# Both third-layer sums of a group added on VectorE, in place of a copy on ScalarE and an addition on GpSimd

## What is computed

```python
x = x + _L0_conv_ref(_ln_c(x), ...)          # sign convolution, batch norm, clip to -1..1
t = _to_tokens(x)                            # one token of 64 channels per point
t = t + _L0_ffn_ref(_ln_t(t), ...)
# inside the second:
w = jax.nn.softmax(feat @ Wr + br, axis=-1)  # feat: mean over the batch
h = relu(_bn(einsum('bfd,edh->bfeh', x, W1) + b1, ...))
h = relu(_bn(einsum('bfeh,ehk->bfek', h, W2) + b2, ...))
y = einsum('bfeh,ehd->bfed', h, Wo) + bo
return einsum('bfed,fe->bfd', y, w)
```

## Time and profile before

| | |
|---|---|
| median of three runs | 1410.8 us |
| the profiled execution | 1413.79 us, span 1411.7 us from the first to the last instruction |
| mean granted TensorE clock | 0.979 of full speed |
| instructions | 36466 |
| DMA | 107.41 MB, mean 76 GB/s |

### The profile page before, as it was taken

The page is one execution under the profiler, slowest core; times in us unless marked ns, Lnnn a source line. Parts: engine busy times, 40 slices in busy tenths (PEclk is TensorE's granted clock), DMA queues, the critical chain, the costliest instruction groups (busy, mean ns, idle before and its releaser), DMA issues.

```text
span 1411.7 us, 36466 instructions
## 1 busy us (share of the span) xinstructions
PE 1326.0 (94%) x14782; PEld 678.3 (48%) x14782; DVE 888.2 (63%) x1592; ACT 868.5 (62%) x1151; POOL 551.2 (39%) x474
## 2 busy tenths in 40 slices
PE   5798946999999999999999999999999999999998
PEld 3675732554444455445444444544454444444443
DVE  3343452666666767666666676667766677766655
ACT  4566654666666666666666666666666666666643
POOL 6104003444434444434444443444443444443441
PEclk9999966999999999999999999999999999999999
DMA  9977512233332323332233333233333232333121
GB/s 200 183 174 163 105 21 53 60 67 74 73 80 48 67 61 74 74 80 52 62 73 67 74 73 61 61 66 67 74 74 74 53 65 62 74 73 77 25 53 28
DMA packets 251026, 107.41 MB, mean 76 GB/s; under 512 B 238865, under 2 KB 239089, under 8 KB 250865
## 3 DMA queue, kind: packets, MB, share of 16 engines
q1 hardware_dynamic: 249600, 103.49, 34.9%
q0 software_dynamic: 1264, 1.61, 0.6%
HBM read 78.97 MB, written 26.09 MB: 74 GB/s over the span
## 4 chain that ended last, share of the span: by engine, by line
PE 92%; issue 3%; DMA 2%; DVE 1%; SPq 1%; ACT 1%; POOL 0%; POOLq 0%; DVEq 0%; ACTq 0%
PE ps L567 25%; PE ps L583 25%; PE ps L545 25%; PE ps L513 7%; PE ps L601 3%; PE ps L498 3%; PE ps L609 2%; PE ps L634 2%; DMA xa<-in_x 2%; PE ps L621 1%; PE ps L628 0%; SPq L266 0%; DMA spread<-rs_rows 0%; DVE bn L872 0%; ACT xc L753 0%
## 5 line engine op out<-in xcount | busy, mean ns | idle before, releaser
L908 DVE SCALAR_TENSOR_TENSOR v<-ps,negb,wb 128x448 f32<-128x448 f32 x896 | 571.0, 678 | 307.4 <-PE ps L567 306.2
L738 ACT ACTIVATE h<-ps,bias 128x896 f32<-128x896 f32 x448 | 451.5, 1008 | 332.1 <-PE ps L545 332.1
L545 PE MATMUL ps<-xc,w 64*64 64x448 f32 x3584 | 468.7, 542 | 15.2 <-POOL xc L422 11.3
L567 PE MATMUL ps<-h,w 64*64 64x448 f32 x3584 | 465.8, 541 | 5.6 <-issue 3.2
L583 PE MATMUL ps<-v,wo 64*64 64x448 f32 x3584 | 466.3, 539 | 3.7 <-issue 2.9
L583 PEld LDWEIGHTS ps<-v,wo 64*64 64x64 f32 x3584 | 179.1, 133 | 179.9 <-issue 160.6
L545 PEld LDWEIGHTS ps<-xc,w 64*64 64x64 f32 x3584 | 165.2, 132 | 189.6 <-issue 182.7
L567 PEld LDWEIGHTS ps<-h,w 64*64 64x64 f32 x3584 | 174.6, 133 | 161.9 <-issue 141.5
L452 POOL TENSOR_TENSOR o<-o,upper 128x448 f32<-128x448 f32 x112 | 127.3, 1137 | 299.8 <-DVE o L918 299.8
L444 POOL TENSOR_TENSOR o<-xin,gconst 128x448 f32<-128x448 f32 x112 | 130.6, 1186 | 235.9 <-ACT gconst L781 143.0
L422 POOL TENSOR_TENSOR xc<-xc,spread 128x896 f32<-128x896 f32 x56 | 123.5, 2221 | 209.9 <-DMA spread<-rs_rows 209.7
(11 more groups left out here) (143 smaller groups left out, 676.6 us busy)
## 6 DMA issues: line engine op xcount, KB each, us to landing
xa<-in_x SPq DMA_DIRECT2D x64, 392.0 KB, 7.4
xin<-in_x SPq DMA_DIRECT2D x112, 224.0 KB, 4.1
spread<-rs_rows SPq DMA_DIRECT2D x112, 224.0 KB, 4.1
out<-o SPq DMA_DIRECT2D x224, 112.0 KB, 2.5
rs_rows<-rs SPq DMA_DIRECT2D x112, 3.5 KB
rows<-in_L_ffn_g POOLq DMA_DIRECT2D x2, 256.0 KB, 12.9
rows<-in_L_ffn_v POOLq DMA_DIRECT2D x2, 256.0 KB, 14.8
cwt<-in_L_conv_weight SPq DMA_DIRECT2D x2, 144.0 KB, 2.7
```

What stands on the lines that cost most here:

```text
L545: last = mm(ps[64 * two:64 * two + 64, L1_BANKS + ab, 0:NG], w1[half, P * q + C * two:P * q + C * two + C], xc[half, s, g // 2, ab ^ (g % ...
L567: last = mm(ps[64 * i:64 * i + 64, L2_BANKS[ab] + low, 0:NG], w2[rows_, Q + QUADS * i, :], h[rows_, u % 2, i, ab, :], start=True, stop=True)
L738: A(h[:, u % 2, i], ps[:, L1_BANKS:L1_BANKS + 2, 0:NG], ACT.Relu, bias=bias[:, 0, q:q + 1]).then_inc(h_done[i], 1)
L908: last = V.scalar_tensor_tensor(out=v[:, u % 2, ab, d, :].rearrange("p (b w) -> p b w", w=W), in0=ps[:, L2_BANKS[ab] + d, 0:NG].rearrange( ...
```

## The change

VectorE now makes both additions of a group, one behind the other, the second behind a semaphore of its own (`lower_in`), since it reads what the first wrote. The ScalarE copy, the tile `upper`, the GpSimd addition and the semaphores `upper_done` and `sum_done` are gone. `out_done` counts the second addition, and TensorE and SyncE wait for it alone. GpSimd keeps `add_const`, `norm` and `feature`.

```diff
@@ store (SyncE)
-                    sp.wait_ge(sum_done, G * k + g + 1)
+                    sp.wait_ge(out_done, G * k + g + 2)
@@ GpSimd
-                def add_upper(k, g):
-
-                    pool.wait_ge(upper_done, G * k + g + 2)
-                    pool.wait_ge(out_done, G * k + g + 2)
-                    og = o[:, BG * g:BG * g + BG, :].rearrange("p b w -> p (b w)")
-                    nc.gpsimd.tensor_tensor(og, og, upper[:], ALU.add).then_inc(sum_done, 1)
-
                 def chunk(k, s, first, left):
-                    for g in range(G - 1):
+                    for g in range(G):
                         add_const(k, s, g)
-                    if not first:
-                        add_upper(k - 1, G - 1)
-                    add_const(k, s, G - 1)
-                    add_upper(k, 0)
                     if left:
                         for p in range(STEPS):
                             norm(k + 1, 1 - s, p)
                         feature(k + 1, 1 - s)
-                    add_upper(k, 1)
-                    add_upper(k, 2)
-                    if not left:
-                        add_upper(k, G - 1)
@@ layer3 (TensorE)
                         if Q == 0:
                             pe.wait_ge(out_done, G * k + g + 1)
-                            pe.wait_ge(upper_done, G * k + g + 1)
@@ ScalarE
-                def take_upper(k, g):
-                    act.wait_ge(l3_done, UNITS * k + QUADS * g + QUADS + RING2)
-                    if not (isinstance(k, int) and k == 0 and g == 0):
-                        act.wait_ge(sum_done, G * k + g)
-                    A(upper[:], ps[:, ACC_BANKS + 1, 0:NG], ACT.Copy).then_inc(upper_done, 1)
@@ add_out (VectorE)
-                    V.tensor_tensor(og, ps[:, ACC_BANKS, 0:NG], og, ALU.add).then_inc(out_done, 1)
+                    V.tensor_tensor(og, ps[:, ACC_BANKS, 0:NG], og, ALU.add).then_inc(lower_in, 1)
+                    dve.wait_ge(lower_in, G * k + g + 1)
+                    V.tensor_tensor(og, ps[:, ACC_BANKS + 1, 0:NG], og, ALU.add).then_inc(out_done, 1)
```

More of the change, by code:

```diff
@@ L113, in metaformer_kernel @@
         vareps = sb("vareps", [P, NG], F32)
-        upper = sb("upper", [P, NG], F32)
         placed = sb("placed", [C, PAIRS * 2, W], F32)
@@ L196, in metaformer_kernel @@
         l3_done = sem("l3_done")
-        upper_done = sem("upper_done")
+        lower_in = sem("lower_in")
         out_done = sem("out_done")
-        sum_done = sem("sum_done")
         stored = [sem(f"stored{g}") for g in range(G)]
@@ L682, in _ @@
             def _(act):
-                for s, n in ((a_signed, 2), (a_kept, 2), (upper_done, 1)):
+                for s, n in ((a_signed, 2), (a_kept, 2)):
                     act.sem_inc(s, n)
@@ L785, in chunk @@
                         following = (k, u + 1) if u + 1 < UNITS else (k + 1, 0)
[L786 to L789, removed]
                         for i in range(2):
@@ L794, in chunk @@
                                 prep_point(prep, k, s, left, POINTS * u + POINTS // 2 * i + p)
-                    if not left:
-                        take_upper(k, G - 1)
                 act.wait_ge(s_bn, 1)
```

## The result

The kernel after takes 1444.5 us (median of 4 runs, 1443.6 to 1446.1), before 1410.6. The ratio is 1.023, interval 1.019 to 1.027: slower by 34 us, where 35 were forecast. The profiled execution of after took 1443.7 us, its span 1441.6; that is 30 us above the span of the profiled execution of before, which lay 3 us above its median.

What follows compares the result with a forecast made beforehand. TensorE, 92% of the chain, was taken as bound, released by VectorE's additions and evictions. Terms 15.1 + 2.2 + 3.1 + 10.5 + 8 - 0.6 - 3 = 35.3 us gave 1446 us, eight-in-ten range 1430 to 1461.

Steps and rivals of the forecast that it cites:

- rival 1: VectorE's idle time covers the second addition, so no change, 1411 us; chance 4%.
- The second addition: On VectorE, per group: 0.61 us of work plus 0.04 for the semaphore wait, 0.65 us more.
- The wait that goes: L583 loses its wait for upper_done; its distance behind the addition falls from 0.21 to 0.10 us.
- u = 3: Unit 3 of a chunk, group 0's sums: L583 bound by the addition in 28 chunks, 0.54 us each, 15.1 us.
- u = 1: Unit 1 of the next chunk, group 3's sums: L609 gives VectorE more time; 26 x 0.12 = 3.1 us.
- The four further places in the last two chunks: Group 3 and group 2 once, group 1 twice, bound as less preparation stands between: 4 x 0.54 = 2.2 us.
- u = 7: Unit 7, group 2's sums: additions delay the gate and the eviction L628 waits for, 0.40 us a chunk, 10.5 us.
- Meetings of L929 with the norm: At u = 4 and 5, VectorE's later third L929 meets GpSimd's L422 in about 21 of 25 chunks: 8 us.
- What is saved: Removed ScalarE and GpSimd work, 188 us, worth only 0.6 us at the end; 3 us of issue stops also covered.
- the 0.6 at the end: At the kernel's end, two VectorE additions finish at 1407.48 instead of GpSimd's addition at 1408.11: -0.6 us.
- The 3 covered: TensorE's issue stops inside chunks, 42 us, partly covered by new waits: 3 us off, between 0 and 8.
- the turn: The L628 matmul at u = 7, waiting for an eviction that comes 0.40 us later: 10.5 us.

Runs made afterwards that it cites:

- no_second: The kernel after without its second VectorE addition, the ScalarE copy and GpSimd addition still gone: 1404.2 us, ratio 0.995.
- only_second: The kernel before with a second VectorE addition appended behind a semaphore, the ScalarE copy and GpSimd addition kept: 1458.1 us, ratio 1.033.

## Why the prediction was right, and where its terms were off

The time (1446 against 1444.5), the sign and the mechanism held. The forecast rested on one reading, that a distance which never varies (0.21 us in 24 chunks) means a release although the list of waits books 0.6 us. The runs bear it out: the distance takes one new value in after (0.257 us, again in 24 chunks), no_second and only_second put the whole loss on the second addition, and rival 1, the cover, is refuted. The reading by occupancy (the Trainium skill, Perfetto Trace Analysis, Identifying the Most-Contended Engine) would have put the time at 1411. The measurement is against it: VectorE went from 63% to 67% of the span, and the time rose by 34 us. By steps:

- The second addition, 0.65 us: right (0.03 + 0.62).
- The wait that goes, -0.11: wrong. L583 was compared with L628 by the number of semaphores, and what counts is the number of wait instructions. Removing upper_done left two instructions, moved out_done out of the second slot of its own, and raised the distance from 0.21 to 0.26, so that the matmul came 0.91 us behind the end of the first addition and not 0.75. So the bound [0.10, 0.21] did not even hold it. This moved u = 3 from 15.1 to 19.1 us and u = 1 from 3.1 to 7.6.
- The four further places in the last two chunks: 2.2 forecast, 2.7 measured.
- u = 7: 10.5 forecast, 7.3 measured over all, 0.35 in the chunk shown where 0.40 was forecast.
- Meetings of L929 with the norm: 8 forecast, 5.3 at and behind both centring blocks. Nearly every chunk met (25, forecast 21), but shorter, because the spread landed 0.7 us earlier. The forecast held the landing fixed; by the code it is tied to GpSimd's lost addition through the store and the load. In only_second, where that link is as before, a meeting lengthens the third x1 operation by 1.4 us on average (34 us over 24).
- What is saved: the 0.6 at the end is right (from the last L918 to the store 1.93 us, from the last L888 to it 1.31). The 3 covered were too little: the removal is worth 8 to 14 us in runs, and the other places came down by 8.0. Some of these 8.0 are shorter stops for instructions (15.1 to 13.2 us); that the rest are the microseconds of the removal is not shown.

So that the total came within 2 us is luck, because errors met: the places u = 3 and u = 1 were put 8.5 us too low (26.7 against 18.2), and the turn, the meetings and what is saved 10.3 us too high (4.6 against 14.9: 7.3 + 5.3 - 8.0 against 10.5 + 8 - 3.6). The margin of the range covered both. These terms account for the 31.3 us of the 27 periods in one execution of each kernel; the medians differ by 34.

## What to carry to other kernels

Where an engine starts at the same distance behind another's end in nearly every round, take it as released by it, whatever the list of waits books; add the new work there at full price.
- A small DRAM round trip (rs out and back) took 3.8 us from issue to issue where two loads of 224 KB had been issued 0.25 us before it, and 2.5 us where they had been issued 1.5 us before. In the medians over 28 chunks it was 3.6 us at 0.2 us (only_second), 2.4 at 1.5 (after) and 2.1 at 1.8 (no_second).
